# One block of attention and a gated mixture of experts in a single kernel: the last expert pair gated on gelu's output, the first two experts image by image, and the orders of all engines rewritten

## What is computed

```python
# x: 4 images, 64 channels, 16x16 pixels (256 tokens an image)
x = x + attention(_ln_c(x))          # single head, d = 16
    q, k, v = wq@x + bq, wk@x + bk, wv@x + bv
    attn = softmax(q^T k)            # 256 x 256 for each image
    out  = v @ attn^T
t = tokens(x)                        # 1024 x 64
t = t + ffn(_ln_t(t))
    xn = layernorm(t)                # of the already normalised tokens
    top2 of softmax(t' @ Wr + br), weights renormalised to sum 1
    h = gelu((xn*ln_g[e] + ln_b[e]) @ W1[e] + b1[e])   # 8 experts, hidden 256
    y = h @ W2[e] + b2[e]
    out = sum over the two chosen e of weight * y
```

## Time and profile before

| what | value |
|---|---|
| median of 3 runs | 62.4 us (62.15 to 62.55) |
| the profiled execution, its own time | 62.13 us |
| its span | 60.2 us |
| granted clock of PE over the span | 1.00 of full speed |
| PE busy | 54.4 us |
| ACT, DVE, POOL busy | 33.4, 31.8, 24.6 us |

### The profile page before, as it was taken

How to read it: one execution, slowest core, us unless ns; L and a number is a source line. 1 busy time by engine, 2 the same in 40 slices (tenths; PEclk the granted TensorE clock), 3 DMA queues, 4 the chain that set the end, 5 groups by cost and what they waited for, 6 DMA issues and landing times.

```text
span 60.2 us, 1140 instructions
## 1 busy us (share of the span) xinstructions
PE 54.4 (90%) x332; PEld 31.4 (52%) x332; DVE 31.8 (53%) x154; ACT 33.4 (56%) x78; POOL 24.6 (41%) x48
## 2 busy tenths in 40 slices
PE   1998999799997999999999995999999999999830
PEld 0323756595865577793453674337374375322730
DVE  2289379729798959863620187822040135333920
ACT  5401458896999447949579049734919649100000
POOL 5157467000166099704609800099617000067300
PEclk9999999999999999999999999999999999999999
DMA  0441557860000000000000066840578300200011
GB/s 0 104 104 24 142 110 298 254 276 6 0 5 0 0 16 0 0 0 0 0 0 11 1 163 212 201 139 16 197 174 212 103 0 0 80 7 0 0 44 44
DMA packets 4309, 4.43 MB, mean 74 GB/s; under 512 B 2188, under 2 KB 2896, under 8 KB 4304
## 3 DMA queue, kind: packets, MB, share of 16 engines
q1 hardware_dynamic: 3984, 4.34, 25.4%
q10 hardware_dynamic: 320, 0.03, 0.5%
HBM read 4.08 MB, written 0.29 MB: 73 GB/s over the span
## 4 chain that ended last, share of the span: by engine, by line
PE 77%; DVE 8%; DMA 3%; issue 3%; ACT 3%; POOL 1%; ACTq 0%; POOLq 0%
PE banks L888 25%; PE banks L913 24%; PE banks L844 7%; PE banks L817 4%; PE banks L798 4%; PE banks L782 3%; DMA X<-in_x_dram 3%; PE banks L866 2%; PE banks L806 2%; DVE gated L662 1%; PE banks L857 1%; POOL rs L287 1%; PE banks L951 1%; PE banks L789 1%; ACT H L428 1%
## 5 line engine op out<-in xcount | busy, mean ns | idle before, releaser
L428 ACT ACTIVATE H<-banks,PF 128x512 f32<-128x512 f32 x32 | 19.8, 685 | 10.1 <-PE banks L888 10.1
L888 PE MATMUL banks<-XE,W1F 64*128 64x256 f32 x128 | 16.6, 393 | 0.7 <-ACT H L428 0.7
L913 PE MATMUL banks<-H,W2F 128*64 128x512 f32 x64 | 15.1, 601 | 0.1
L888 PEld LDWEIGHTS banks<-XE,W1F 64*128 64x128 f32 x128 | 11.7, 186 | 6.2 <-issue 5.2
L323 POOL TENSOR_TENSOR acc<-acc,gated 128x512 f32<-128x512 f32 (+1 forms) x6 | 6.5, 1087 | 13.8 <-DVE gated L662 13.8
L309 POOL TENSOR_SCALAR XE<-XF,PF,LB 128x256 f32<-128x256 f32 x15 | 8.2, 559 | 4.1 <-ACT XF L409 4.1
L662 DVE SCALAR_TENSOR_TENSOR gated<-banks,B2T,GS 128x512 f32<-128x512 f32 (+1 forms) x7 | 4.6, 673 | 7.4 <-PE banks L913 7.4
L293 POOL TENSOR_TENSOR rs<-base,half 128x4 f32<-128x4 f32 x4 | 4.1, 1027 | 9.6 <-DVE base L571 9.6
L913 PEld LDWEIGHTS banks<-H,W2F 128*64 128x64 f32 x64 | 4.1, 136 | 7.4 <-issue 7.4
L782 PE MATMUL banks<-zeros 128*128 128x512 f16 x17 | 6.8, 523 | 1.3 <-POOL zeros L326 1.3
L844 PE MATMUL banks<-V,PTS 128*128 128x64 f32 x32 | 4.3, 277 | 0.1
(11 more groups left out here) (81 smaller groups left out, 60.1 us busy)
## 6 DMA issues: line engine op xcount, KB each, us to landing
GS<-gates_kept SPq DMA_DIRECT2D x16, 128.0 KB, 3.0
W1F<-in_w_dram SPq DMA_DIRECT2D x1, 768.0 KB, 4.4
W2F<-in_w_dram SPq DMA_DIRECT2D x1, 512.0 KB, 4.8
W1F<-in_w_dram SPq DMA_DIRECT2D x1, 256.0 KB, 3.2
out_dram<-res SPq DMA_DIRECT2D x4, 64.0 KB, 1.6
X<-in_x_dram SPq DMA_DIRECT2D x2, 64.0 KB, 2.0
X<-in_x_dram SPq DMA_DIRECT2D x1, 128.0 KB, 2.5
WQK<-in_attn_w_dram ACTq DMA_DIRECT2D x2, 16.0 KB, 2.2
```

What stands on the lines that cost most here:

```text
L428: nc.scalar.activation(H[:, r, :].rearrange("p (t n) -> p t n", t=PT), ps_z[g // J % 2][:, :, PIX * j:PIX * j + PIX], ACT.Gelu, bias=PF[:, ...
L888: nc.tensor.matmul(ps_z[q % 2][:, k, PIX * j:PIX * j + PIX], W1F[rows, e, j, :], XE[h][rows, e, :], start=True, stop=True).then_inc(z_read ...
L913: mm = nc.tensor.matmul(ps_y[s % 2][C * k:C * k + C, :], W2F[:, u, :], H[:, (2 * J * s + J * k + j) % RING, :], start=(j == 0), stop=(j == ...
```

## The change

1. The last pair (experts 6 and 7 of half 1). Their gates are applied to gelu's output: `G7` holds each row of gates over 128 partitions, `weigh_last(n)` multiplies four 128x512 blocks of `H` into `HG`, and layer 2 of the pair runs in two calls, `layer2_last(0)` and `(1)`, of 256 columns each. Its bias is added to the tokens ahead of time in the token layout (`last_bias`, eight instructions of 128x64). `add_third` adds the third pair's product on DVE, `add_last(k)` forms the sum for each 256 columns, `fold_last(k)` and `finish_last(k)` end it.
2. `layer1_first(q, i)` replaces layer1(0) and layer1(1): experts 0 and 1 of half 0, an image (128 columns of each row group) at a time. ACT still stretches for expert 0, POOL for expert 1 by image (`stretch_second`). Expert 0 has a pair of banks of its own (4 and 5), so three experts' outputs stand before the first gelu has to be read.
3. Scores of images 2 and 3 are issued together, image 3 on row groups 64 to 127 (`QS`, `KS` are laid out on 128 partitions).
4. `second_pow` now has two columns and `router_pow(h)` the four of the router.
5. The lists of all engines are rewritten. Two of the three `keep_warm` pieces behind the first attention images are gone. `layer2(1)` moves behind `layer1(8)`, `turn_x2(3)` ahead of `layer1(5)`, `turn_gates(1)` behind `layer1(10)`, `fold_sum` ahead of `layer1(14)`.

```diff
-        ps_z = [banks[:, k:k + PT, :] for k in (1, 6)]
+        ps_z = [banks[:, k:k + PT, :] for k in (4, 1, 6)]
...
+            sp.dma_start(B2R[:, :, :], b2[0, E - 2:E, :].partition_broadcast(P)).then_inc(b2r_in, 16)
...
+                    if s == STEPS - 1:
+                        sp.dma_start(G7[:, k, :], gates_kept[h, 2 * p + k, :].partition_broadcast(P)).then_inc(g7_in, 16)
...
             def second_pow(i):
-                nc.gpsimd.tensor_tensor(rs2[h][:, :, im], base2[h][:, :, im], half[:, :, :], ALU.pow)\
+                nc.gpsimd.tensor_tensor(rs2[h][:, 0, im], base2[h][:, 0, im], half[:, 0, :], ALU.pow)\
...
+            def router_pow(h):
+                pool.wait_ge(varr_ready, IMG * (h + 1))
...
+            def stretch_second(i):
+                pool.wait_ge(XF_ready, i + 1)
+                nc.gpsimd.tensor_scalar(XE[0][:, 1, P * i:P * i + P], XF[0][:, i, :],
+                                        PF[:, F_G + 1:F_G + 2], LB[:, 1:2], ALU.mult, ALU.add).then_inc(xe_second, 1)
...
+            def weigh_last(n):
+                dve.wait_ge(g7_in, 32)
+                dve.wait_ge(h_ready, HALVES * UNITS - 2 * J + n + 1)
+                nc.vector.tensor_tensor(HG[:, n, :], H[:, (HALVES * UNITS - 2 * J + n) % RING, :], G7[:, n // J, :],
+                                        ALU.mult).then_inc(hg_ready, 1)
...
+                for n in range(TILES):
+                    t = tile_of(n)
+                    last = nc.vector.scalar_tensor_tensor(out=T7[k][:, t, :], in0=B2R[:, k, :],
+                                                          scalar=gate[1][:, n, E - 2 + k:E - 1 + k],
+                                                          in1=src[:, t, :], op0=ALU.mult, op1=ALU.add)
...
+            def add_third():
+                dve.wait_ge(acc_ready, PAIRS)
+                dve.wait_ge(gated_ready, STEPS - 1)
+                nc.vector.tensor_tensor(acc[1][:, :], acc[1][:, :], gated[0][:, :], ALU.add).then_inc(third_ready, 1)
+            def add_last(k):
+                dve.wait_ge(last_ps, 2 * (k + 1))
+                dve.wait_ge(third_ready, 1)
+                nc.vector.tensor_tensor(last_sum[k][:, :], ps_last[k], acc[1][:, PIX * k:PIX * k + PIX], ALU.add)\
...
+            def layer1_first(q, i):
+                pe.wait_ge(w1_in[0], 16)
+                if q == 0:
+                    pe.wait_ge(xe_first, i + 1)
...
+                for j in range(J):
+                    for k in range(PT):
+                        rows = slice(C * k, C * k + C)
+                        nc.tensor.matmul(ps_z[z_slot(q)][:, k, PIX * j + P * i:PIX * j + P * i + P], W1F[rows, q, j, :],
+                                         XE[0][rows, q, P * i:P * i + P], start=True, stop=True)\
+                            .then_inc(z_first[q], 1)
...
+            def layer2_last(c):
+                pe.wait_ge(hg_ready, 2 * J)
+                if c == 0:
+                    pe.wait_ge(gated_ready, STEPS - 2)
+                else:
+                    pe.wait_ge(h_ready, HALVES * UNITS)
+                for j in range(J):
+                    for k in range(2):
+                        mm = nc.tensor.matmul(ps_last[c][C * k:C * k + C, :], W2F[:, J * (E - 2 + k) + j, :],
+                                              HG[:, J * k + j, PIX * c:PIX * c + PIX],
+                                              start=(j == 0), stop=(j == J - 1))
```

More of the change, by code:

```diff
@@ L85, in build_block @@
         ps_out = banks[:, 3, :].rearrange("p (t k c) -> p t k c", t=TILES, k=2)
+        ps_last = [banks[:, k, 0:PIX] for k in (0, 6)]
         ps_end = [banks[:, k, 0:IMG * C].rearrange("p (t c) -> p t c", t=IMG) for k in (3, 1)]
@@ L224, in build_block @@
         gateT_ready = sem("gateT_ready")
+        xe_second = sem("xe_second")
+        z_first = [sem(f"z_first{q}") for q in range(2)]
         z_ready = sem("z_ready")
@@ L339, in _ @@
             first_pow(2)
+            add_bias(0)
             first_pow(3)
-            add_bias(0)
-            add_bias(1)
             second_pow(0)
             second_pow(1)
-            stretch(0, 1)
-            stretch(0, 2)
+            router_pow(0)
+            stretch_second(0)
+            add_bias(1)
+            stretch_second(1)
+            for e in range(2, 6):
+                stretch(0, e)
             second_pow(2)
-            for e in range(3, 7):
-                stretch(0, e)
             second_pow(3)
+            router_pow(1)
+            stretch(0, 6)
             stretch(0, 7)
-            for e in range(0, 5):
+            for e in range(0, 4):
                 stretch(1, e)
             add_up(1)
-            for e in range(5, 8):
-                stretch(1, e)
+            stretch(1, 4)
+            stretch(1, 5)
             add_up(2)
+            stretch(1, 6)
             add_up(3)
+            stretch(1, 7)
             add_up(5)
-            add_up(6)
         @block.scalar
@@ L741, in _ @@
             route(0, 0)
-            second_moments(2)
+            second_variance(2)
             route(0, 1)
-            second_variance(2)
-            for stage in range(2, 5):
-                route(0, stage)
             second_norm(2)
+            sum_tokens(3)
+            route(0, 2)
+            second_stats(3)
+            route(0, 3)
+            route(0, 4)
+            second_moments(3)
+            second_variance(3)
             route(0, 5)
+            route(1, 0)
+            second_norm(3)
@@ L749, in _ @@
             route(0, 6)
-            sum_tokens(3)
-            second_stats(3)
-            second_moments(3)
             route(0, 8)
-            second_variance(3)
             route(0, 7)
-            second_norm(3)
             route(0, 9)
             route(0, 10)
-            for stage in range(0, 6):
+            for stage in range(1, 11):
                 route(1, stage)
-            route(1, 8)
-            route(1, 6)
-            route(1, 7)
-            route(1, 9)
-            route(1, 10)
@@ L766, in _ @@
             weigh(0)
+            last_bias(0)
             weigh(1)
             weigh(2)
+            last_bias(1)
             weigh(3)
             weigh(4)
-            finish(0)
+            finish_part()
+            weigh_last(0)
+            weigh_last(1)
+            finish_first()
+            weigh_last(2)
             weigh(5)
+            weigh_last(3)
             weigh(6)
-            weigh(7)
-            add_last()
-            finish(1)
+            add_third()
+            add_last(0)
@@ L778, in _ @@
+            add_last(1)
+            finish_last(0)
+            finish_last(1)
         @block.tensor
@@ L967, in _ @@
             turn_x1(2)
+            scores(1)
             values(1)
-            scores(1)
+            turn_x1(3)
             queries_keys(2)
-            turn_x1(3)
             turn_probs(0)
-            keep_warm(3, 1)
             queries_keys(3)
+            turn_probs(1)
             attend(0)
-            turn_probs(1)
-            scores(2)
+            scores(2, 3)
             values(2)
-            scores(3)
+            values(3)
             attend(1)
@@ L982, in _ @@
             turn_b2()
-            values(3)
             turn_probs(3)
@@ L1005, in _ @@
             layer1(8)
+            layer2(1)
             layer1(9)
+            layer1(10)
             turn_gates(1)
             layer2(2)
-            layer1(10)
             layer1(11)
@@ L1014, in _ @@
             layer2(4)
+            fold_sum()
             layer1(14)
             layer1(15)
-            fold_sum()
             layer2(5)
             layer2(6)
-            layer2(7)
-            fold_even()
-            fold_odd()
+            layer2_last(0)
+            layer2_last(1)
+            fold_last(0)
+            fold_last(1)
 _OUTS = [((P, IMAGES * PT, C), 'float32')]
```

259 lines of the change are left out of this document (138 added, 121 removed).

## The result

The changed kernel takes 60.55 us (median of 4 runs, 59.97 to 61.6) where the kernel before took 62.3 (4 runs). The ratio of the two is 0.969, with a 95% interval of 0.962 to 0.977: 3.1% faster. (Single executions of most kernels here lie up to 2 us above their lowest; the ratios leave disturbed ones out.) The forecast was 61.3 us, 0.85 less than the profiled execution. That execution of the changed kernel took 60.08 us with a span of 58.2: 2.05 less than before. The direction was right, the size 0.85 of the 2.05 us that came.

A forecast was written before the change was run, and what follows sets the result against it. TensorE, busy 90% of the span, was taken as the bound. The sum was 0.85 us less, the tail giving 0.9 and gates and DVE's row taking 0.8 back: 62.13 - 0.85 = 61.3 us, range 60.4 to 62.8.

The forecast's parts named there:

- The wait at layer1(9): TensorE's wait of 0.71 us for gelu, until 36.94, is filled by layer2(1) moved behind layer1(8): 0.7 gained.
- Passes of 128 columns: First two experts by image: calls of 0.47, four taking 1.9 us against 2.03, so no cost in itself.
- Rival (b): Weight loads not hidden beside the 128-column passes, 0.12 more for each of 16 pairs: 62.3 to 62.8 us; chance 0.06.
- The front: Up to layer 1: its first image starts at 20.25 and not 20.72, gain 0.45 us, bounds nothing and 0.7.
- The middle: To the end of layer1(10): gain 1.2 us, from 0.75 start and blocks, 0.7 wait, less 0.25 small new waits.
- The last pair: Doubled gates land at 49.4, DVE then has no gap, and layer2_last(0) starts at 53.5, not 52.7.
- The tail: Behind the last product: one sum and not three operations, would give 0.9 us; last addition ends at 57.3.
- Rival (a): POOL's add_up(5) starts ahead of weigh_last(3), which waits up to 1.27 us: 62.1 us; chance 0.12.
- Rival (c): Gates landing after 49.4 delay layer2_last(0) one to one; two us late are 63.3 us; chance 0.15.
- Rival (e): Gates in time and no DVE/POOL lock: layer2_last(0) starts at 52.7, total 60.3 us; chance 0.10.

The follow-up runs named there:

- u_image: Changed kernel with experts 0 and 1 each in one go of 256 columns, both images awaited, and no dummy matmuls; ratio to the kernel before 0.987.
- g_late: Changed kernel with two more 128 KB transfers, into an unused tile, ahead of those of G7; 61.1 us against 62.33 for the kernel before.
- ff_late: Changed kernel with finish_first moved behind weigh_last(3) on DVE; ratio to the kernel before 0.970.
- b_order: Kernel before with one call moved, layer2(1) behind layer1(8); 61.12 us, ratio to the kernel before 0.988.
- u_scores: Changed kernel with the joined scores of images 2 and 3 issued as scores(2), values(2), scores(3), values(3); ratio to the kernel before 0.975.
- u_tail: Changed kernel with the last pair as before (layer2(7), weigh(7) in halves, gates on 64 partitions), all else kept; ratio to the kernel before 0.974.

## Why the prediction was wrong where it was

*The wait at layer1(9).* Right: 0.7 forecast, 0.63 to 0.9 measured, alone and undone.

*Passes of 128 columns.* Nearly right. The weight loads do run beside passes on the same rows: 24 passes in 1.61, 0.067 each, so a call of eight is 0.54 and not 0.47. Rival (b) (0.24 a pair) is out. By image, layer 1 starts 0.85 earlier and takes 0.35 longer: net 0.5. I had put the start to 0.45 for the front as a whole, and this edit's part in it was most of that.

*The front.* This is the first step that failed: "layer 1 starts at 20.25". It started at 19.48. At scores(0) I was at 8.15 and the kernel at 7.80. I carried 0.23 of the vector engine's delay through to there. The first transposition was indeed 0.19 later (5.26 for 5.07), but then the three dummies took 0.92 where they had taken 1.22, and that is nearly all of the 0.35. As far as their pace tells, it is the moment at which TensorE comes to full speed, which one execution can't forecast. Between scores(0) and layer 1 I had 12.10 and it took 11.68: exps(1) ended at 11.5, and I had it end at 12.15, 0.3 later than the delay at scores(0) explains. On that chain ACT starts each instruction some 0.1 before the last one's end (the copy of X1T of 0.26 at 10.33, the next at 10.47), and I added full durations. Layer 1's start gained 1.24 and not 0.45, which split into 0.12 at scores(0), 0.27 from all other edits of the front together (12.80 against 12.53 in u_image; 0.13 of it is what the joined scores are worth), and 0.85 by image.

*The middle.* Right in kind. From the start of attend(3) (1.28 ahead) to the start of layer1(9) (35.25 against 36.94: 1.69) the kernel gained 0.41: the wait of 0.7 less 0.3. Most of that 0.3 is in two rows: turn_x2(2) and (3) now both stand by themselves (0.26 each, where one had 0.12 in company), and so does turn_gates(0) (0.21 for 0.11). I had 0.25 for small losses.

*The last pair.* This is the second step that failed: "layer2_last(0) starts at 53.5, not 52.7". The mechanism was right (g_late, u_image, ff_late), the size of the wait was not: 0.19 and not 0.8. The row began at 48.57 and not at 49.4. The gates' transfers began 0.59 earlier with all the rest (40.25 for 40.84), and the two large ones took 3.4 to 3.9 from issue to landing, where I had allowed more than 4. What then held the row was as much gelu(28) as the gates. And the row took 3.55 and not 4.1, because I added rounded durations where instructions that I had at 0.7 start 0.60 to 0.66 apart. TensorE itself was ready at 51.98 and not 52.7, by the front. So layer2_last(0) started 1.33 earlier than forecast, 0.72 from TensorE's lead and 0.61 from the wait. The calls took 0.10 more than forecast and the tail 0.06 less, and the last addition ended 1.29 earlier (56.01 for 57.3).

*The tail.* I had 1.95 from the end of the last product to the end of the last addition; it took 1.89 (54.12 to 56.01). The "0.9" that the prediction gives to the tail itself doesn't follow from its own clock times, which make it 0.45 (2.40 to 1.95); 0.51 is what came. I had a delay of add_up(5) by weigh_last(3) of 0.7: it was 0.38 (1.65 for 1.27), and add_third waited 0.31 for it, without effect on the end.

*The rivals.* Rival (a) didn't happen: DVE's instruction was first, as argued. (Its price was summed too low: it moved layer2_last(0) by 1.15 and the end by 0.8 only.) Rival (c) has the mechanism of g_late; without added transfers the gates came just in time. Rival (e) (60.3) came nearest in time, and I gave it one in ten. It wasn't the outcome as it stands: DVE was late by 0.19, POOL was held, and the front, which (e) leaves as forecast, gave the larger share.

Both errors point the same way: sums of many small pieces, each rounded to the safe side.

## What to carry to other kernels

Where two engines meet within a fraction of a us, add up their rows by pitches (start to start) and not by durations. Read a wait in the same way: compare the distance between two starts with that in a kernel in which nothing has to wait, for a modelled end of a pass can hide 0.2 us. An order that fills a known wait is the cheapest edit there is: one moved line gave 1.2% of 3.1. A transfer that is doubled at the end of a queue can cost nothing and still leave the kernel hanging on its landing, one for one, as soon as it is later than what else is awaited.

## What the runs showed of the hardware

The pace of TensorE's passes doubles at a point that differs from one execution to another, in kernels that start in the same way. The kernel before and b_order start alike: three dummies of 512 columns took 1.22 us in one profile and 0.81 in the other, and scores(0) came at 7.92 and 7.49. In the eight profiles that start as the changed kernel does it was 0.81 to 1.01, with scores(0) at 7.55 to 7.96. So some 0.4 us of difference between two profiled executions can be that alone. The distance from scores(0) to layer 1 repeats to 0.02.

Products on four row groups ran beside each other without a price: 8 passes in 0.71, where 4 took 0.70 on two row groups (by the timelines of the changed kernel and of u_scores).

A POOL addition of 128x512 took 1.65 where a DVE instruction with two SBUF inputs had started 0.16 ahead of it. It took 1.26 or 1.27 for the earlier pairs, and 1.27 for this same pair in u_tail, which has no such DVE instruction.

From SP's write of the gates to DRAM to the first transfer that reads them back it took 2.0 to 3.1 us in thirteen profiles of one piece of code. And in the one profiled execution in which TensorE waited 2.1 us near the end, its granted clock was 0.50 for the rest.
